# A causal attention loop on one core: weighted values two steps behind, and each score bank filled beside the other half's first-pass unit

## What is computed

```python
scores = jnp.einsum('bhqd,bhkd->bhqk', q, k) / hd ** 0.5
causal = jnp.tril(jnp.ones((S, S), dtype=bool))
scores = jnp.where(causal, scores, -jnp.inf)
attn = jax.nn.softmax(scores, axis=-1)
o = jnp.einsum('bhqk,bhkd->bhqd', attn, v).transpose(0, 2, 1, 3).reshape(B, S, D)
```

## Time and profile before

| | us |
|---|---|
| median of 3 timed runs | 3980.94 (3979.54 to 3983.21) |
| profiled execution, its own time | 3961.53 |
| its span | 3959.8 |
| TensorE busy | 3253.9 (82%) |
| VectorE busy | 2989.6 (75%) |
| ScalarE busy | 2556.4 (65%) |
| the causal loop in it | 789.2 to 1242.0 |

### The profile page before, as it was taken

How to read it: one execution, slowest core, us unless ns; L and a number is a source line. 1 busy time by engine, 2 the same in 40 slices (tenths; PEclk the granted TensorE clock), 3 DMA queues, 4 the chain that set the end, 5 groups by cost and what they waited for, 6 DMA issues and landing times. The chain is left out here.

```text
span 3959.8 us, 130158 instructions
## 1 busy us (share of the span) xinstructions
PE 3253.9 (82%) x55226; PEld 2131.1 (54%) x55226; DVE 2989.6 (75%) x3700; ACT 2556.4 (65%) x4943; POOL 607.0 (15%) x1597
## 2 busy tenths in 40 slices
PE   2999999489996996564955459999999999999628
PEld 1666666245554773122543436666666666666414
DVE  5999998468893114997353369999999999999653
ACT  1899999357775443331211139999999999999622
POOL 0000010021000000662012011111111111111220
PEclk7999999789998997997957769999999999999858
DMA  4000000300000000530019865555545555554410
GB/s 116 9 8 9 10 7 5 104 14 11 9 5 10 19 16 27 191 127 6 1 27 180 247 152 125 121 129 123 132 120 130 124 126 128 120 134 116 105 33 11
DMA packets 209578, 305.81 MB, mean 77 GB/s; under 512 B 93116, under 2 KB 137602, under 8 KB 207950
## 3 DMA queue, kind: packets, MB, share of 16 engines
q1 hardware_dynamic: 202270, 286.06, 28.8%
q10 hardware_dynamic: 2048, 6.29, 0.7%
q0 software_dynamic: 4688, 5.24, 0.6%
HBM read 228.17 MB, written 60.40 MB: 73 GB/s over the span
## 5 line engine op out<-in xcount | busy, mean ns | idle before, releaser
L862 ACT ACTIVATE channels_qk<-psum 128x512 f32<-128x512 f32 (+1 forms) x3906 | 2095.6, 595 | 260.5 <-PE psum L705 183.5
L924 DVE TENSOR_REDUCE l2f_chunk_max<-psum 128x2 f32<-128x1024 f32 x1176 | 1360.4, 1219 | 61.3 <-PE psum L680 52.7
L924 DVE TENSOR_REDUCE chunk_max<-psum 128x2 f32<-128x1024 f32 (+2 forms) x832 | 916.8, 1157 | 105.8 <-PE psum L680 59.4
L680 PE MATMUL psum<-l2f_k_parts,l2f_q_parts 48*128 48x512 bf16 x2352 | 716.2, 388 | 43.1 <-DVE l2f_chunk_max L924 31.9
L726 PE MATMUL psum<-channels_qk,l2f_v_and_ones 128*9 128x128 f32 x18432 | 718.2, 274 | 12.5 <-issue 12.3
L705 PE MATMUL psum<-l2f_q_parts,l2f_k_parts 51*128 51x128 bf16 x9224 | 727.4, 218 | 0.5 <-ACT l2f_minus_max_rows L904 0.4
L705 PEld LDWEIGHTS psum<-l2f_q_parts,l2f_k_parts 51*128 51x128 bf16 x9224 | 496.7, 94 | 32.2 <-ACT channels_qk L862 23.6
L680 PE MATMUL psum<-k_parts,q_parts 48*128 48x512 bf16 (+3 forms) x1664 | 425.0, 383 | 97.4 <-DMA q_parts<-q_rows_dram 67.7
L726 PE MATMUL psum<-channels_qk,v_and_ones 128*9 128x128 f32 x12544 | 492.7, 275 | 0.6 <-ACT channels_qk L862 0.5
L726 PEld LDWEIGHTS psum<-channels_qk,l2f_v_and_ones 128*9 128x9 f32 x18432 | 397.3, 90 | 121.0 <-issue 16.1
L705 PE MATMUL psum<-q_parts,k_parts 51*128 51x128 bf16 x6272 | 432.7, 219 | 30.8 <-DMA q_parts<-minus_max_rows 10.4
(11 more groups left out here) (479 smaller groups left out, 3234.3 us busy)
## 6 DMA issues: line engine op xcount, KB each, us to landing
l2f_k_parts<-l2f_k_parts_dram SPq DMA_DIRECT2D x604, 192.0 KB, 3.7
l2f_v_and_ones<-expert_v_dram SPq DMA_DIRECT2D x148, 288.0 KB, 4.1
l1a_bc_rows<-ssm_rows_dram SPq DMA_DIRECT2D x32, 512.0 KB, 4.7
expert_v_dram<-l2f_v_and_ones SPq DMA_DIRECT2D x8, 1152.0 KB, 4.4
channels_qk<-ssm_rows_dram SPq DMA_DIRECT2D x16, 512.0 KB
expert_q_dram<-heads_out SPq DMA_DIRECT2D x8, 1024.0 KB, 7.5
l2f_q_parts<-l2f_gathered_q_parts SPq DMA_DIRECT2D x456, 16.0 KB
k_parts<-k_rows_dram ACTq DMA_DIRECT2D x32, 192.0 KB, 6.2
```

The costliest lines, as they stand in the source:

```text
L680: last = nc.tensor.matmul(c.ps[:, 2 * (n % 2) + j, 0:width], at.q[64 * j:64 * j + ROWS, tile % SLOTS, pair, :], kx(tile)[64 * j:64 * j + R ...
L862: nc.scalar.activation(at.prob[:, s % 4, j, 0:kts, :].rearrange("p k q -> p (k q)"), c.ps[:, ring.bank(i, n), 0:kts * 2 * P], ACT.Exp, sca ...
L924: v.tensor_reduce(at.mx[:, 4 * g + 2 * pp:4 * g + 2 * pp + 2, chunk], c.ps[:, 2 * (n % 2):2 * (n % 2) + 2, 0:span.width(tile, chunk)], X, ...
```

## The change

In `causal_tile`, the values move to the head of a step and go two steps back: step s - 2 in step s, and the last two steps of a tile in the first two of the next. The first unit of a step is issued by halves, half 1, then half 0, with the scores of step s + 1 between and behind them by halves, 0, then 1. A second unit of the step comes after both, its halves together. After the loop two steps of values are left instead of one. Every matmul and every wait of the others is kept; only TensorE's order and the places of its waits change.

```diff
--- before.py
+++ after.py
@@ -767,36 +767,35 @@
                     pe.wait_ge(mparts_ready, (i + ahead) * G + (group + 1))
                     turn_rows(group, ring.bank(i, n)).then_inc(s2_ready, 1)
 
+            def values_of(s, i):
+                pe.wait_ge(s2_read, ring.read_when(i, ring.place(i, (s, 1))))
+                weighted_values(s, i)
+
             def causal_tile(i):
                 steps = span.steps(i)
                 last_step = G * steps - 1
                 for s in range(G * steps):
                     g, u = s // steps, s % steps
                     group, tile = first_pass_of(i, g)
-                    if exists(tile):
-                        for unit in share(2 * span.chunks(tile), u, steps):
-                            first_pass(group, unit, tile)
-                    if s < last_step:
-                        second_pass(s + 1, (0, 1), i)
+                    if s < 2 and i > 0:
+                        values_of(G * span.steps(i - 1) - 2 + s, i - 1)
+                    if s == 3:
+                        pe.wait_ge(oT_copied, i + 1)
+                        values_of(0, i)
+                    if s >= 3:
+                        values_of(s - 2, i)
+                    units = share(2 * span.chunks(tile), u, steps) if exists(tile) else []
+                    for j in range(2):
+                        for unit in units[:1]:
+                            first_pass(group, unit, tile, (1 - j,))
+                        if s < last_step:
+                            second_pass(s + 1, (j,), i)
+                    for unit in units[1:]:
+                        first_pass(group, unit, tile)
                     for name in ring.due(i, s):
                         side_work(i, g, name)
                     if s == last_step and exists(i + 1):
                         second_pass(0, (0, 1), i + 1)
-                    if s == 0 and i > 0:
-                        before = G * span.steps(i - 1) - 1
-                        pe.wait_ge(s2_read, ring.read_when(i - 1, ring.place(i - 1, (before, 1))))
-                        weighted_values(before, i - 1)
-                    if s == 2:
-                        pe.wait_ge(oT_copied, i + 1)
-                        pe.wait_ge(s2_read, ring.read_when(i, ring.place(i, (0, 1))))
-                        weighted_values(0, i)
-                    if s >= 2:
-                        pe.wait_ge(s2_read, ring.read_when(i, ring.place(i, (s - 1, 1))))
-                        weighted_values(s - 1, i)
-
-            def values_of(s, i):
-                pe.wait_ge(s2_read, ring.read_when(i, ring.place(i, (s, 1))))
-                weighted_values(s, i)
 
             def full_tile(i):
 
@@ -844,8 +843,7 @@
                 pe.wait_ge(s2_read, ring.read_when(done, closed - ring.size))
             else:
                 pe.wait_ge(s2_read, ring.read_when(tiles - 1, closed))
-            if tri is None:
-                weighted_values(before - 1, tiles - 1)
+            weighted_values(before - 1, tiles - 1)
             weighted_values(before, tiles - 1)
             turn_out(done, ring.place(tiles, "out"))
             if routed:
```

## The result

The changed kernel took 4019.31 us in the median (4014.7 to 4029.57), the kernel before 3981.74 beside it: a ratio of 1.0091, 95% interval 1.0075 to 1.0107. It is 37.6 us slower, where +14 with a range up to +35 was forecast. The direction was right, the size was not.

The account below looks back on a forecast made before the run. TensorE was taken to bound the middle tiles (94% busy), though not alone. The terms +42 - 26 - 4 + 4 gave +16 us, taken as +14: median 3995 us, range 3970 to 4016.

Parts of the forecast that it names:

- The prices of steps: TensorE in the causal loop: plain step 1.10 us in both orders; step with a paired 512-column diagonal unit 2.06 against 1.43.
- the sum: Whole change: +42 - 26 - 4 + 4 = +16 us, then taken as +14.
- Waits given back in tiles 2 to 14: Waits of TensorE for ScalarE and VectorE that the new order saves: -26 us, bounds 0 and 56.
- late next: VectorE expected to be the next engine to hold TensorE once ScalarE's waits go.
- The unmasked tile: Earlier attention loop already in the new order: VectorE busy 36.89 of 37.7 us, where 32 steps x 1.10 would be 35.2.
- The split masks' price: Tiles 2 to 14, TensorE's added work from masks between halves: diagonal units 33.4, masked scores 10.4, second units -2; +42 us.
- Tiles 0 and 1: Work put between the row maxima's wait and the turning of rows delays the next step: +4 us, bounds 0 and +8.
- The chain: Tiles 0 and 1: from scores to TensorE reaching the rows 3.1 us, 1.2 beyond the old 1.94, in five steps.
- Tile 15: Last tile, no first pass left: 28 plain steps save 0.17 us each, masked ones give 1 back; -4 us, bounds 0 and -6.
- rival A: Split masks cost nothing extra because the weight load before a mask is hidden: sum +3, median 3984; chance 0.23.
- B: Most of ScalarE's and VectorE's waits are given back, 56 of 56 us: sum -16, median 3965; chance 0.15.
- C: Later row maxima count in tiles 0 to 3 and half the waits return as VectorE's: +33, median 4014; chance 0.14.

Follow-up runs that it names:

- unit_masks_split: Changed kernel, but steps with masked scores keep both halves together while masked units are still split; ran once, loop 456.0 us against 450.3 before.
- masked_together: Changed kernel, but steps whose unit or scores carry a mask keep both halves together; 3970.93 us, ratio 0.9963 to the kernel before.
- light_together: masked_together with VectorE's maximum in the causal loop taken over half of each unit's columns; ran once, loop 422.4 us.
- small_old: Changed kernel with crosswise pairing only from tile 4 on, tiles 0 to 3 in old pairs; 4013.14 us in one run, loop 471.7.
- masks_last: Changed kernel with both halves' masks issued behind both halves of unit and scores; 3949.2 us, ratio 0.9953 to the kernel before.
- pairing_only: Changed kernel with halves paired crosswise but the values left one step behind; 4023.64 us, ratio 1.0099 to the kernel before.

## Why the prediction was wrong in size

**What held.** That TensorE bounds the middle tiles and that only waits could be won there. The prices of steps: 1.10 plain, 2.06 (measured 2.07) with a split mask. A step with masked scores takes 1.64 us when split and 1.43 in pairs, 0.21 more, priced 0.2: first the changed kernel, then unit_masks_split, both in tile 13.

```profile
1162.81 0.39 PE L680 MATMUL psum<-k_parts,q_parts 48*128 48x512 bf16 x1
...
1164.45 0.39 PE L680 MATMUL psum<-k_parts,q_parts 48*128 48x512 bf16 x1
```

```profile
1150.40 0.39 PE L680 MATMUL psum<-k_parts,q_parts 48*128 48x512 bf16 x2
...
1151.83 0.39 PE L680 MATMUL psum<-k_parts,q_parts 48*128 48x512 bf16 x1
```

Also held: that tiles 6, 10 and 14 grow by some 3 us (4.9, 2.9, 3.6), that L705's waits for ScalarE vanish (4.0), and that moved values are free. The loop grew by 33.9 us where the sum has +16: 10.8 of the difference lie in tiles 2 to 14, 5.2 in tiles 0 and 1, and 1.8 in tile 15.

**The step that failed: "Waits given back in tiles 2 to 14 ... I take 26".** It was 8.8 (masked_together: 8.6 in tiles 4 to 14, 0.2 in tiles 2 and 3). The sign that I had named for it failed as well: tiles 7 and 11, where no unit's pair is parted by a mask, were to be 2 to 4 us shorter, and came out 1.4 longer and 0.4 shorter. I took it near ScalarE's 30 us, because that row names the wait that the change removes. It does name it, and the wait went. But TensorE then came earlier to the slots of the first pass, and VectorE, busy for 86%, empties them no faster: 12 of 20 us stand again as L680 waiting for VectorE. With VectorE light the same edit gives 16.8 in tiles 4 to 14, still short of 26; in light_together L705 still waits 12.9 us for ScalarE. I had named VectorE as late next and then priced that at 4 us. The unmasked tile had a hint of it: 2.5 us over its 35.2 us of work, while VectorE is busy for 36.89 of 37.7. I did not carry it over to the causal tiles.

**The split masks' price, +42,** was nearly right as work on TensorE: with VectorE light 28.6 us of time and 33.3 of busy time, for 35 in tiles 4 to 14. In the loop's length it came out at 32.1 in tiles 2 to 14, tile 3's clock left out (30.8 in tiles 4 to 14). This error had the other sign.

**Tiles 0 and 1: +4, measured +9.2.** The chain and its length were right (3.1 us to the rows, 3.14 measured); the steps that I read in both tiles lost 1.5 us each, and I had counted five, at 1.2, and then discounted tile 0, which alone lost 5.5. **Tile 15: -4, measured -2.2** with a clock of 0.95 there. In small_old, with the same order and a clock of 1.00, it is -3.3, in masks_last -4.1.

**The clock was not in the sum.** Tile 3's 3.5 us are a fall to the lower level that before did not have.

Of the rivals, A fell with the masked step: the mask starts 0.32 us behind its half unit in the new order as well (1202.34 to 1202.66), so it does not follow as soon as the 0.21 us of columns have streamed. The prediction gave rival A the sentence of the Trainium skill ("TensorE: Matmul & The Clock Gate", Part 3, The mechanism) by which a load for other rows or for the background buffer is pulled ahead. The same section also says that loads overlap matmuls in flight only when their row group differs. The 0.32 us fit this second sentence, as the mask's weights go to rows that the half unit is using. The four scores of one half do not fit it: each has a load of its own to the same rows, and the next line starts 0.24 us after the first of them (1202.82 to 1203.06), hardly more than the 0.213 us of their 512 columns. So neither sentence alone gives both rows. B did not come. C is nearest to what came, +33 for 33.9, in part by luck. Its 13 us of waits won are nearest to the measured 8.8. The small tiles grew by 13.8 us, but 9.2 of these are tiles 0 and 1 and 3.5 the clock, while tile 2, where C had later row maxima too, grew by 1.1.

## What to carry to other kernels

When an edit removes the wait that a row names, ask when the engine then reaches its next semaphore and how busy the one behind it is: the crosswise pairs are worth 16.8 us here with VectorE light and 8.6 with its full load. Interleaving work that shares the array by rows paid here only where nothing that takes all rows came between the halves (masked_together, masks_last); put such pieces at the end of the interleaved group. And a pattern that is right for one loop should be costed on the steps that only the other loop has. When two causes are tried apart, look which steps have both: here eight had, and neither kernel touched them.

## What the runs showed of the hardware that I had not expected

A half unit of 48 rows and the mask of 128 rows behind it start 0.32 us apart for 512 columns, which are 0.213 us at 2.4 GHz. A mask of 128 columns (0.053 us) and the scores of 51 rows behind it start 0.15 to 0.16 us apart. Both hold in the old order and in the new. So each change between part and all of the array's rows cost about 0.1 us over the stream.

The granted clock went to its lower level for stretches of 3 to 10 us in the midst of a loop in which TensorE is busy for 94%, and in pairing_only it was still there through tile 2, which then took 27.7 us in place of 17.2. Falls in tiles 2, 3, 11 and 15 came in some kernels and not in others. Tile 7 has one in eight of the fourteen profiles, and in none with VectorE light.
